# Product-key experts on one core: matmul blocks of one kind in stretches of four, weights in pairs between them

## The chip, the cores and the metric

The kernel runs on one core of a Trainium2 chip. The metric is the device time of one execution in microseconds (us), the median of several runs. A NeuronCore has a matrix engine (TensorE, PE in the profile, with its weight loads as PEld), a vector engine (VectorE, DVE), a scalar engine (ScalarE, ACT), a general engine (GpSimd, POOL) and an engine that starts transfers (SyncE, SP). Each works through its own queue in order; they meet at semaphores. TensorE writes only to PSUM, here eight banks of 128 x 512 float32.

## The reference

The program is a block of four layers over x (4 sequences of 512 tokens, 256 features): two attentions with gates, a mixture of head experts, and at the end the product-key experts, which is the stage that this change touches:

```python
xn = _rmsnorm(x, norm_w)                       # after a layer norm
q = (xn @ w_q.T).reshape(b, t, H, 2, DK)       # H = 8 heads
sim1 = jnp.einsum('bthd,hkd->bthk', q[..., 0, :], keys[:, :, 0, :])   # 64 keys
sim2 = jnp.einsum('bthd,hkd->bthk', q[..., 1, :], keys[:, :, 1, :])
s1, i1 = jax.lax.top_k(sim1, K)                # K = 8
s2, i2 = jax.lax.top_k(sim2, K)
all_sc = (s1[..., :, None] + s2[..., None, :]).reshape(b, t, H, K * K)
fs, pk = jax.lax.top_k(all_sc, K)              # 8 of 64 pairs
fi = jnp.take_along_axis(all_idx, pk, axis=-1) # one of 4096 experts
hidden = jax.nn.gelu(jnp.einsum('btd,bthkd->bthk', xn, expert_down[fi]))
hidden = hidden * jax.nn.relu(fs)
return jnp.einsum('bthk,bthkd->btd', hidden, expert_up[fi])
```

Each token so picks 64 experts of 4096, each with one row of a down and one row of an up matrix.

## The kernel before

The expert stage (`product_key_experts`) gathers nothing. It runs in 16 turns, one for each tile of 128 tokens, and computes the hidden value of **all** 4096 experts, multiplies it by a dense matrix of weights that is zero where an expert was not picked, and multiplies the product by the up matrix. The 4096 experts are 128 x 32: 32 columns j, in eight blocks of four.

TensorE's work of a turn i (function `turn` of the tensor block, L2465):

- `hidden(i + 1, ..., n)`, n = 0 to 7, L2423: block n of down matrix times the normed tile of the **next** turn, in float32, 8 matmuls of 128 columns; the trace has 16 instructions for them. It writes one of two banks in turn, and waits until ScalarE has taken that bank's last block through the gelu.
- `weights(i, n)`, L2440: 24 matmuls in bfloat16, 64 columns each. They turn the picks of 16 tokens (n picks the 16) into their dense weights, from one-hot matrices that VectorE made. Blocks 2c and 2c+1 use the one-hots `c` (0 to 3), for which there are two buffers. The result goes to one of three banks, and a block waits until VectorE has used that bank's last content.
- `spend(i - 1, ..., n)`, L2450: block n of weighted hidden values of the **last** turn times the up matrix, float32, 4 matmuls of 256 columns, 8 instructions in the trace. Block 0 waits for the last multiplication of the turn before.
- `turn_x(i + 2)` (L2387), the transposing of the tile after the next, and `compare(i + 2)` (L2397), its similarities with all keys, 8 instructions of 512 columns, which use the two banks of `hidden`. So `hidden` 4 and 5 wait until ScalarE has copied them. ScalarE in its turn copies them only when `largest_places` of tile i + 1 has ended.
- `turn_picks(i + 1)` (L2407): the transposing of the next tile's picks. It waits for the last step of the ranking (43 steps, the last at L2277).

VectorE's work of a turn (L2630): `apply(i, n)` (L2603), the multiplication of weights block n with the hidden values; `onehots(i, 2)` and `(i, 3)`, and at the end those of the next turn, `(i + 1, 0)` and `(i + 1, 1)`, after `split_score(i + 1)` (L2564, L2567); one-hots are three instructions (L2580, L2585, L2591). `update` (L2609) adds a finished tile to x. The ranking `topk` has six parts: part 0 is `largest` (16 MAX8, L2191) for tile i + 2; parts 1 to 5, for tile i + 1, are `largest_places` (16 searches, L2287), and the four parts of `rank`: 2 (pair sums and 8 MAX8, from L2240), 3 (8 searches from L2252, then small steps to L2259), 4 and 5 (L2228, L2233, L2235 each; 5 ends at L2277). In turns 2 to 9 the layer norm of the last batch lies here too, one part a turn (`late`).

The last turns differ by `ahead`, the number of tiles that are still ahead: turn 15 has no `hidden`, no comparison and no ranking, and after it the eight `spend` of tile 15 follow. Turn 0 has no `spend`.

The order is written out by hand. TensorE's in a middle turn is, before the change, with H, S, W for the three kinds of block, X, C, P for `turn_x`, `compare`, `turn_picks`:

H0 S0 S1 H1 W0 W1 S2 H2 W2 S3 H3 W3 X S4 C W4 H4 S5 H5 W5 S6 H6 W6 S7 H7 P W7

Of the kernel before, what the change touches and what calls it, by code (L numbers as in the profile page):

```python
# [25 lines left out]
B, S, D = 4, 512, 256  # L26
# [89 lines left out]
def build(nc, a, out):  # L116
    with ExitStack() as ctx:
# [41 lines left out]
        b_attention(nc, a, m)  # L159
        c_attention(nc, a, m)  # L160
        product_key_experts(nc, a, m)
        epilogue(nc, out, m)

# [2127 lines left out]
def product_key_experts(nc, a, m):  # L2291
# [10 lines left out]
    NB, BP = 8, 8  # L2302
# [14 lines left out]
    e = m["D"]  # L2317
# [10 lines left out]
    c_out, c_y, c_bo = m["C.out_made"], m["work"][:, 15616:15872], m["work"][:, 15872:16128]  # L2328
    every_other = ident.rearrange("p (n two) -> p two n", two=2)
    SELECT, PICK = 3, 7  # L2330
    late, LATE, LATE_FROM = e.norm, 4, 2

    with ExitStack() as ctx:
        def sig(what, per):
# [2 lines left out]
        def sem(what):  # L2337
            return ctx.enter_context(nc.semaphore("D_" + what))

        consts, c_added = sem("consts"), sem("last_attention_added")  # L2340
# [14 lines left out]
        with nc.Block() as block:  # L2355
# [24 lines left out]
            def _(eng):  # L2380
                def turn_x(i):

                    eng.wait_ge(staged.sem, staged.at(i, 1))
                    if i == 1:
                        eng.wait_ge(selt_ready.sem, selt_ready.at(0, 2))
                    for c in range(KC):
                        last = eng.transpose(XP[:, c * P:(c + 1) * P], xstage[:, c * P:(c + 1) * P], ident[:, :])  # L2387
                    last.then_inc(xt_made.sem, 1)

                def compare(i, par):  # L2390

                    eng.wait_ge(xt_ready.sem, xt_ready.at(i, 1))
                    if i >= 2:
                        eng.wait_ge(h_ready.sem, h_ready.at(i - 1, SELECT + 1))
                    for n in range(2):
                        for kc in range(KC):
                            last = eng.matmul(WP[n] if i == 1 else HP[n][:, :], xnT[par][:, kc, :], simw[:, kc, n * 512:(n + 1) * 512],  # L2397
                                              start=(kc == 0), stop=(kc == KC - 1))
                        last.then_inc(sim_made.sem, 1)
# [11 lines left out]
                def hidden(i, par, n):  # L2411

                    if i and i < NT - 1 and n in (SELECT + 1, SELECT + 2):
                        eng.wait_ge(sim_ready.sem, sim_ready.at(i + 1, n - SELECT))
                    if i == 0 and n % 2 == 0:
                        eng.wait_ge(s[f"down_loaded_{n // 2}"], 16)
                    if n >= 2:
                        eng.wait_ge(h_ready.sem, h_ready.at(i, n - 1))
                    elif h_ready.due(i - 1, ELO // NJ - 1 + n):
                        eng.wait_ge(h_ready.sem, h_ready.at(i - 1, ELO // NJ - 1 + n))  # L2420
                    for q in range(NJ):
                        for kc in range(KC):
                            last = eng.matmul(HP[n % 2][:, q * P:(q + 1) * P], down[:, (n * NJ + q) * KC + kc, :],  # L2423
                                              xnT[par][:, kc, :], start=(kc == 0), stop=(kc == KC - 1))
                    last.then_inc(h_made.sem, 1)

                def weights(i, n):

                    if n % 2 == 0:
                        eng.wait_ge(hot_ready.sem, hot_ready.at(i, n // 2 + 1))  # L2430
                    if n >= 3:
                        eng.wait_ge(g_ready.sem, g_ready.at(i, n - 2))
                    elif g_ready.due(i - 1, (7, 8, 6)[n]):
                        eng.wait_ge(g_ready.sem, g_ready.at(i - 1, (7, 8, 6)[n]))
                    c = n // 2 % 2
                    for q in range(BP):
                        at = n % 2 * BP + q
                        dst = WP[n % 3].rearrange("p (j t) -> p j t", t=TW)[:, :, 2 * q:2 * q + 2]
                        for f in range(3):
                            last = eng.matmul(dst, hot[:, c, at, :], lot[c][:, at, f, :], start=(f == 0), stop=(f == 2))  # L2440
                    last.then_inc(w_made.sem, 1)

                def spend(i, par, n):

                    if n == 0:
                        eng.wait_ge(g_ready.sem, g_ready.at(i, NB))
                        if turn_done.due(i - 2, 1):
                            eng.wait_ge(turn_done.sem, turn_done.at(i - 2, 1))
                    for j in range(n * NJ, (n + 1) * NJ):
                        last = eng.matmul(UPP[par][:, 0:D], G[par][:, j, :], up[:, j, :],  # L2450
                                          start=(j == 0), stop=(j == ELO - 1))
                    if n == NB - 1:
                        last.then_inc(up_made.sem, 1)
# [9 lines left out]
                eng.wait_ge(sim_ready.sem, sim_ready.at(1, 2))  # L2463

                def turn(i, par, ahead):  # L2465
                    for n in range(NB):
                        if n == 0 and ahead >= 1:
                            hidden(i + 1, 1 - par, n)
                        if i:
                            spend(i - 1, 1 - par, n)  # L2470
                        if n == SELECT + 1:
                            if ahead >= 2:
                                compare(i + 2, par)
                            weights(i, n)
                        if n and ahead >= 1:
                            hidden(i + 1, 1 - par, n)
                        if n == PICK and ahead >= 1:
                            turn_picks(i + 1)
                        if n == 1:
                            weights(i, 0)  # L2480
                        if n and n != SELECT + 1:
                            weights(i, n)
                        if n == SELECT and ahead >= 2:
                            turn_x(i + 2)

                turns(turn)
                for n in range(NB):
# [58 lines left out]
            def _(eng):  # L2546
# [4 lines left out]
                def topk(i, part):  # L2551

                    if part == 0:
                        largest(eng, m, i)
                    elif part == 1:
                        largest_places(eng, m, i)
                    else:
                        rank(eng, m, i, part, selt_made)
# [37 lines left out]
                def apply(i, par, n):  # L2596

                    if n == 0:
                        eng.wait_ge(h_ready.sem, h_ready.at(i, NB))
                        if up_made.due(i - 2, 1):  # L2600
                            eng.wait_ge(up_made.sem, up_made.at(i - 2, 1))
                    eng.wait_ge(w_made.sem, w_made.at(i, n + 1))
                    eng.tensor_tensor(G[par][:, :, n * TW:(n + 1) * TW], WP[n % 3].rearrange("p (j t) -> p j t", t=TW),  # L2603
                                      Hg[par][:, :, n * TW:(n + 1) * TW], ALU.mult).then_inc(g_ready.sem, 1)

                def update(i, par):
                    eng.wait_ge(up_made.sem, up_made.at(i, 1))
                    xt = x[:, i, :]
                    eng.scalar_tensor_tensor(out=xt, in0=UPP[par][:, 0:D], scalar=gate, in1=xt, op0=ALU.mult, op1=ALU.add  # L2609
                                             ).then_inc(turn_done.sem, 1)  # L2610
# [13 lines left out]
                onehots(0, 1)  # L2624
                topk(1, 0)
                topk(1, 1)
                PARTS = {0: 1, 1: 2, 2: 3, 4: 4, 5: 5}
                FIRST_PARTS = {0: 2, 2: 3, 4: 4, 5: 5}

                def turn(i, par, ahead):  # L2630
                    for n in range(NB):
                        apply(i, par, n)
                        if n in (1, 3):
                            onehots(i, 2 + n // 2)
                        if n == 2 and i >= 2:
                            update(i - 2, par)
                        parts = PARTS if i else FIRST_PARTS
                        if ahead >= 1 and n in parts:
                            topk(i + 1, parts[n])
                        if n == LATE and LATE_FROM <= i < LATE_FROM + late.parts:  # L2640
                            if i == LATE_FROM:
                                eng.wait_ge(c_added, 2)
                            late.on_vector(eng, B - 1, i - LATE_FROM)
                        if ahead >= 2 and n == PICK - 1:
                            topk(i + 2, 0)
                        if ahead >= 1 and n == PICK:
                            split_score(i + 1)
                            onehots(i + 1, 0)
                            onehots(i + 1, 1)

                turns(turn)
                update(NT - 2, 0)
# [46 lines left out]
```

## Time and profile before

| what | value |
|---|---|
| runs | 2201.64, 2198.76, 2201.66 us; median 2201.64 |
| the profiled execution | 2201.63 us, its span 2199.8 us, mean granted clock 0.998 |
| TensorE busy | 2140.0 us, 97% of the span |
| VectorE busy | 1671.2 us, 76% |
| ScalarE busy | 791.6 us, 36% |
| expert stage | from about 1592 us to the end |

How to read it: an engine's rows carry the start and the duration of an instruction or of a merged run of them. Matmuls are pipelined, so the duration of one is longer than its distance from the next; how long a block holds TensorE is the distance from its start to the start of what follows. A row's bracket names the idle time before it and the instruction that ended it. "PEclk" is the granted TensorE clock as a share of 2.4 GHz.

### The profile page before, as it was taken

To read this page: it belongs to the slowest core of one execution; us is meant where nothing else is said; L and a number is where in the kernel's file an instruction comes from. 1 tells how busy PE (TensorE), PEld (TensorE's weight loads), DVE (VectorE), ACT (ScalarE), POOL (GpSimd) and SP (SyncE) were. 2 spreads that over 40 slices of the span, in tenths; PEclk is the share of its full clock that TensorE was granted. 3 is DMA by queue.
4 is the path that set the end of the run, shared out by engine and by line. 5 is a ranking of instruction groups with operands and counts; after the bars stand their busy time and mean duration, and the time that the engine had idled before them with its cause. 6 is when DMAs were issued, how large, how long until landed. Compare 5 with 4: busy or idle time off the path is not lost. (4 is left out here: it accounts for less than half of the span.)

```text
span 2199.8 us, 44678 instructions
## 1 busy us (share of the span) xinstructions
PE 2140.0 (97%) x17740; PEld 1443.5 (66%) x17740; DVE 1671.2 (76%) x4463; ACT 791.6 (36%) x1687; POOL 270.2 (12%) x515
## 2 busy tenths in 40 slices
PE   7999989999999999999999999999999999999998
PEld 3555544446746746775556555556689989898997
DVE  6888886776576576536887787877788988889896
ACT  4877772312302302303554554555422111211210
POOL 4866643000000000000000001000000000000000
PEclk9999999999999999999999999999999999999999
DMA  5112104000000003001000000001200000000000
GB/s 181 33 46 52 34 22 158 1 1 1 1 0 1 1 1 115 1 1 51 1 1 1 1 1 1 1 1 51 94 12 2 2 11 2 1 11 1 2 11 10
DMA packets 26207, 50.66 MB, mean 23 GB/s; under 512 B 6032, under 2 KB 14480, under 8 KB 24976
## 3 DMA queue, kind: packets, MB, share of 16 engines
q1 hardware_dynamic: 26000, 47.81, 6.6%
q8 instruction: 141, 2.31, 0.4%
q14 instruction: 66, 0.54, 0.1%
HBM read 37.57 MB, written 2.10 MB: 18 GB/s over the span
## 5 line engine op out<-in xcount | busy, mean ns | idle before, releaser
L2423 PE MATMUL banks<-work,big 128*128 128x128 f32 x2016 | 247.5, 276 | 0.9 <-DMA big<-in_D_up 0.9
L626 ACT ACTIVATE work<-banks,work 128x512 f32<-128x512 f32 x256 | 174.8, 687 | 202.2 <-DVE work L746 202.2
L2423 PEld LDWEIGHTS banks<-work,big 128*128 128x128 f32 x2016 | 241.3, 192 | 5.9 <-DMA big<-in_D_up 1.1
L1121 PE MATMUL banks<-big,work 128*128 128x256 f32 x1024 | 241.2, 379 | 0.0
L1045 PE MATMUL banks<-big,work 128*128 128x512 f32 x512 | 226.6, 596 | 0.0
L2520 ACT ACTIVATE work<-banks 128x512 f32<-128x512 f32 x126 | 75.3, 597 | 398.5 <-PE banks L2423 398.5
L1121 PEld LDWEIGHTS banks<-big,work 128*128 128x128 f32 x1024 | 195.0, 190 | 33.9 <-issue 1.9
L1045 PEld LDWEIGHTS banks<-big,work 128*128 128x128 f32 x512 | 95.5, 190 | 113.8 <-issue 112.8
L1963 ACT ACTIVATE work<-work 128x512 f32<-128x512 f32 x256 | 164.3, 711 | 0.1
L746 DVE TENSOR_REDUCE work<-banks 128x2 f32<-128x1024 f32 x128 | 150.5, 1217 | 7.7 <-PE banks L478 7.7
L1343 DVE CUSTOM_DVE_ANT_0 work<-banks,work 128x512 f32<-128x512 f32 (+3 forms) x128 | 57.6, 488 | 121.5 <-PE banks L1061 109.4
L1872 PEld LDWEIGHTS banks<-ident,work 64*128 64x128 f32 x2048 | 76.4, 140 | 99.9 <-ACT work L1963 69.4
L494 PEld LDWEIGHTS banks<-ident,work 64*128 64x128 f32 x2048 | 74.0, 139 | 89.1 <-issue 51.5
L1228 ACT ACTIVATE work<-work 128x512 f32<-128x512 f32 (+3 forms) x128 | 70.8, 554 | 168.4 <-DVE work L1343 168.3
L1312 DVE TENSOR_TENSOR work<-banks,work 128x512 f32<-128x512 f32 x128 | 87.9, 690 | 52.1 <-PE banks L1045 51.6
L478 PE MATMUL banks<-work 64*128 64x256 f32 x1024 | 124.6, 383 | 0.9 <-DVE work L739 0.9
L2450 PE MATMUL banks<-big,wab 128*128 128x256 f32 x512 | 122.6, 385 | 0.8 <-DVE wab L2603 0.8
L2450 PE MATMUL banks<-big,work 128*128 128x256 f32 x512 | 121.2, 384 | 0.8 <-DVE work L2603 0.8
L507 PE MATMUL banks<-big,wc 128*64 128x512 f32 x512 | 116.9, 598 | 3.4 <-ACT wc L647 2.9
L764 DVE COPY big<-banks 128x512 f32<-128x512 f32 x128 | 87.7, 685 | 38.9 <-PE banks L494 38.7
L755 DVE TENSOR_SCALAR work<-work 128x512 f32<-128x512 f32 x256 | 113.0, 484 | 4.5
L2591 DVE TENSOR_TENSOR wc<-wc,work 128x3072 bf16<-128x3072 bf16 x64 | 112.1, 1752 | 0.0
(256 smaller groups left out, 3782.1 us busy)
## 6 DMA issues: line engine op xcount, KB each, us to landing
work<-work SPq DMA_DIRECT2D x168, 32.0 KB, 2.0
big<-in_bias SPq DMA_DIRECT2D x16, 256.0 KB, 3.6
big<-in_B_val SPq DMA_DIRECT2D x8, 512.0 KB, 5.4
big<-in_B_out SPq DMA_DIRECT2D x1, 4096.0 KB, 16.7
big<-in_D_downT SPq DMA_DIRECT2D x4, 1024.0 KB, 5.6
big<-in_D_up SPq DMA_DIRECT2D x1, 4096.0 KB, 15.6
wc<-in_ctxT SPq DMA_DIRECT2D x1, 2048.0 KB, 8.0
wab<-in_L_ffn_w_q SPq DMA_DIRECT2D x1, 2048.0 KB, 9.5
```

Of the source, the lines that this page charges most:

```text
L478: last = eng.matmul(SB[i][:, j, c * 256:(c + 1) * 256], qT[r, t % 2, qt * P:(qt + 1) * P], kT[r, t % 2, c * 256:(c + 1) * 256], start=True ...
L507: last = eng.matmul(FB[0][j * DK:(j + 1) * DK, :], vtok[:, kt, h * DK:(h + 1) * DK], pT[:, (t % 2 * PAIR + j) * QT + kt, :], start=(kt == ...
L626: eng.activation(prob[:, n % NS * PAIR + j, :], SB[n % 2][:, j, :], ACT.Exp, bias=low[:, n % NS, j:j + 1], accum_out=rowsum[:, n % NS, j:j ...
L746: eng.tensor_reduce(low[:, n % NS, :], SB[n % 2], AX.X, ALU.max, negate=True).then_inc(low_ready.sem, 1)
L755: last = eng.tensor_scalar(one, one, rinv[:, n % NS, j:j + 1], None, ALU.mult)
L1045: last = eng.matmul(value_bank(b, n), xnT[:, kc, t * P:(t + 1) * P], w_val[:, kc, h * EB * DK:(h + 1) * EB * DK], start=(kc == 0), stop=(k ...
L1121: last = eng.matmul(XO[qt // 2][:, qt % 2 * D:(qt % 2 + 1) * D], spread[:, c % NG, qt * P:(qt + 1) * P], w_out[:, c, :], start=False, stop ...
L1312: eng.tensor_tensor(scaled[:, n % NG, :].rearrange("p (k e) -> p k e", e=EB), value_bank(b, n).rearrange("p (k e) -> p k e", e=EB), gm[:, ...
L1963: eng.activation(one, one, ACT.Exp, bias=low[:, n % 2, j:j + 1], scale=-1.0).then_inc(p_ready, 1)
L2423: last = eng.matmul(HP[n % 2][:, q * P:(q + 1) * P], down[:, (n * NJ + q) * KC + kc, :], xnT[par][:, kc, :], start=(kc == 0), stop=(kc == ...
L2450: last = eng.matmul(UPP[par][:, 0:D], G[par][:, j, :], up[:, j, :], start=(j == 0), stop=(j == ELO - 1))
L2591: eng.tensor_tensor(lot[b].rearrange("p n f (j two) -> p n f j two", two=2), elo[:, b].rearrange("p n (j two) -> p n j two", two=2).unsque ...
```

## The change

TensorE's turn is put in two halves of four blocks each. In a half, four H stand together, then two W, then four S, then two W. `turn_x` stands behind W1, the comparison behind S3, `turn_picks` behind S7. In the letters from above a middle turn is then:

H0 H1 H2 H3 W0 W1 X S0 S1 S2 S3 C W2 W3 H4 H5 H6 H7 W4 W5 S4 S5 S6 S7 P W6 W7

VectorE's turn is dealt in pairs to match: multiplications 0 and 1, one-hots 2, parts 1 and 2 of the ranking; multiplications 2 and 3, one-hots 3, the update, part 3; multiplications 4 and 5, parts 4 and 5, the layer norm's part, part 0 of the tile after the next; multiplications 6 and 7, the score's split and two one-hots. ScalarE's code is the same, and so is every instruction of TensorE and VectorE; only their order in the queues changes. The diff, with a constant that is no longer used left out:

```diff
                 def turn(i, par, ahead):
-                    for n in range(NB):
-                        if n == 0 and ahead >= 1:
-                            hidden(i + 1, 1 - par, n)
-                        if i:
-                            spend(i - 1, 1 - par, n)
-                        if n == SELECT + 1:
-                            if ahead >= 2:
-                                compare(i + 2, par)
-                            weights(i, n)
-                        if n and ahead >= 1:
-                            hidden(i + 1, 1 - par, n)
-                        if n == PICK and ahead >= 1:
-                            turn_picks(i + 1)
-                        if n == 1:
-                            weights(i, 0)
-                        if n and n != SELECT + 1:
-                            weights(i, n)
-                        if n == SELECT and ahead >= 2:
-                            turn_x(i + 2)
+                    for half in (range(NB // 2), range(NB // 2, NB)):
+                        for n in half:
+                            if ahead >= 1:
+                                hidden(i + 1, 1 - par, n)
+                        weights(i, half[0])
+                        weights(i, half[1])
+                        if half[0] == 0 and ahead >= 2:
+                            turn_x(i + 2)
+                        for n in half:
+                            if i:
+                                spend(i - 1, 1 - par, n)
+                        if half[0] == 0 and ahead >= 2:
+                            compare(i + 2, par)
+                        if half[0] and ahead >= 1:
+                            turn_picks(i + 1)
+                        weights(i, half[2])
+                        weights(i, half[3])
...
-                PARTS = {0: 1, 1: 2, 2: 3, 4: 4, 5: 5}
-                FIRST_PARTS = {0: 2, 2: 3, 4: 4, 5: 5}
-
                 def turn(i, par, ahead):
-                    for n in range(NB):
-                        apply(i, par, n)
-                        if n in (1, 3):
-                            onehots(i, 2 + n // 2)
-                        if n == 2 and i >= 2:
-                            update(i - 2, par)
-                        parts = PARTS if i else FIRST_PARTS
-                        if ahead >= 1 and n in parts:
-                            topk(i + 1, parts[n])
...
+                    apply(i, par, 0)
+                    apply(i, par, 1)
+                    onehots(i, 2)
+                    if ahead >= 1:
+                        if i:
+                            topk(i + 1, 1)
+                        topk(i + 1, 2)
+                    apply(i, par, 2)
+                    apply(i, par, 3)
+                    onehots(i, 3)
+                    if i >= 2:
+                        update(i - 2, par)
+                    if ahead >= 1:
+                        topk(i + 1, 3)
+                    apply(i, par, 4)
+                    apply(i, par, 5)
+                    if ahead >= 1:
+                        topk(i + 1, 4)
+                        topk(i + 1, 5)
+                    if LATE_FROM <= i < LATE_FROM + late.parts:
...
+                    if ahead >= 2:
+                        topk(i + 2, 0)
+                    apply(i, par, 6)
+                    apply(i, par, 7)
+                    if ahead >= 1:
+                        split_score(i + 1)
+                        onehots(i + 1, 0)
+                        onehots(i + 1, 1)
```

## Rows read from the trace of the kernel before

**Rows 1.** The page's first part: busy time, share of the span, instructions.

```profile
span 2199.8 us, 44678 instructions
PE 2140.0 (97%) x17740; PEld 1443.5 (66%) x17740; DVE 1671.2 (76%) x4463; ACT 791.6 (36%) x1687; POOL 270.2 (12%) x515
```

**Rows 2.** Busy time by stretch; behind the engines the granted clock, DMA share, GB/s.

```profile
1640.00:2120.00 480.00, 480.00 (x5060) 430.49 (x5059) 417.54 (x1496) 94.22 (x188) 5.84 (x26) 1.00 0.02 5
2160.00:2199.80 39.80, 34.60 (x320) 29.67 (x320) 21.45 (x29) 0.00 (x0) 0.00 (x0) 1.00 0.04 14
```

**Rows 3.** The waits of TensorE from 1600 us on: total, times, longest.

```profile
PE banks L2440 <- DVE wc L2591: 1.0, 1, 1.0
```

**Rows 4.** Timeline of TensorE, a middle turn: start, duration, line, shapes, count.

```profile
1893.73 2.03 PE L2423 MATMUL banks<-work,big 128*128 128x128 f32 x16
1895.60 3.62 PE L2450 MATMUL banks<-big,work 128*128 128x256 f32 x16
1899.05 1.95 PE L2423 MATMUL banks<-work,big 128*128 128x128 f32 x16
1900.84 1.56 PE L2440 MATMUL banks<-wc 128*128 128x64 bf16 x48
1902.24 1.97 PE L2450 MATMUL banks<-big,work 128*128 128x256 f32 x8
1904.05 1.95 PE L2423 MATMUL banks<-work,big 128*128 128x128 f32 x16
...
1929.12 1.95 PE L2423 MATMUL banks<-work,big 128*128 128x128 f32 x16
1931.00 0.57 PE L2407 MATMUL banks<-ident,work 128*64 128x64 f32 x12
...
1932.21 1.92 PE L2423 MATMUL banks<-work,big 128*128 128x128 f32 x15
```

**Rows 5.** Timeline of TensorE, turn 0 and the start of turn 1.

```profile
1602.35 1.56 PE L2440 MATMUL banks<-wc 128*128 128x64 bf16 x48
...
1608.88 0.42 PE L2387 MATMUL banks<-ident,work 128*128 128x128 f32 x2
...
1614.25 3.82 PE L2423 MATMUL banks<-work,big 128*128 128x128 f32 x32
1617.90 0.86 PE L2440 MATMUL banks<-wc 128*128 128x64 bf16 x24
...
1624.35 2.03 PE L2423 MATMUL banks<-work,big 128*128 128x128 f32 x16
```

**Rows 6.** Timeline of VectorE, turn 0.

```profile
1603.93 0.68 DVE L2240 TENSOR_TENSOR wab<-work 128x512 f32<-128x512 f32 x1
...
1609.81 0.68 DVE L2603 TENSOR_TENSOR wab<-banks,work 128x512 f32<-128x512 f32 x1
...
1612.71 0.68 DVE L2603 TENSOR_TENSOR wab<-banks,work 128x512 f32<-128x512 f32 x1
...
1617.31 0.42 DVE L2228 TENSOR_TENSOR wab<-work 128x512 bf16<-128x512 bf16 x1
...
1622.07 0.69 DVE L2603 TENSOR_TENSOR wab<-banks,work 128x512 f32<-128x512 f32 x1
```

**Rows 7.** Timeline of TensorE, end of turn 14, turn 15 and after it.

```profile
2158.80 0.87 PE L2440 MATMUL banks<-wc 128*128 128x64 bf16 x24
2160.46 3.72 PE L2450 MATMUL banks<-big,wab 128*128 128x256 f32 x16 [0.78 <-DVE wab L2603]
2165.21 1.57 PE L2440 MATMUL banks<-wc 128*128 128x64 bf16 x48 [1.03 <-DVE wc L2591]
...
2182.82 14.08 PE L2450 MATMUL banks<-big,work 128*128 128x256 f32 x64 [0.78 <-DVE work L2603]
```

**Rows 8.** Early in the first attention: TensorE's timeline, then busy time by stretch.

```profile
32.52 1.12 PE L1872 MATMUL banks<-ident,work 64*128 64x64 f32 x16 [1.21 <-ACT wc L1957]
...
33.00:39.00 6.00, 6.00 (x39) 3.07 (x37) 4.68 (x13) 4.08 (x7) 0.00 (x0) 0.50 0.69 218
```

More of the change, by code:

```diff
@@ L2330, in product_key_experts @@
     SELECT, PICK = 3, 7
-    late, LATE, LATE_FROM = e.norm, 4, 2
+    late, LATE_FROM = e.norm, 2
     with ExitStack() as ctx:
@@ L2626, in _ @@
                 topk(1, 1)
-                PARTS = {0: 1, 1: 2, 2: 3, 4: 4, 5: 5}
-                FIRST_PARTS = {0: 2, 2: 3, 4: 4, 5: 5}
                 def turn(i, par, ahead):
-                    for n in range(NB):
-                        apply(i, par, n)
-                        if n in (1, 3):
-                            onehots(i, 2 + n // 2)
-                        if n == 2 and i >= 2:
-                            update(i - 2, par)
-                        parts = PARTS if i else FIRST_PARTS
-                        if ahead >= 1 and n in parts:
-                            topk(i + 1, parts[n])
[L2640 to L2649, printed above, removed]
+                    apply(i, par, 0)
@@ new lines, in turn @@
+                    apply(i, par, 5)
[3 more added lines that the diff above has]
+                    if LATE_FROM <= i < LATE_FROM + late.parts:
+                        if i == LATE_FROM:
+                            eng.wait_ge(c_added, 2)
+                        late.on_vector(eng, B - 1, i - LATE_FROM)
+                    if ahead >= 2:
+                        topk(i + 2, 0)
+                    apply(i, par, 6)
+                    apply(i, par, 7)
```

## The prediction

> **What bounds the kernel now.** I read four views in this order. The page's first part: TensorE is busy 2140.0 us of a span of 2199.8 us [rows 1]. The busy time by stretch: from 1640 to 2120 us, twelve and a half turns of the expert stage, TensorE is busy 480.00 of 480.00 us at a granted clock of 1.00, VectorE 417.54 us (87%) and ScalarE 94.22 us (20%) [rows 2]. The reader is to see that no engine but TensorE sets the pace there, and that VectorE is near enough to take over. The waits from 1600 us on: TensorE waits for VectorE's one-hots 1.0 us in all [rows 3]. Last the timeline of TensorE in one turn, where starts can be subtracted. One turn goes from 1893.73 to 1932.21, 38.48 us [rows 4], and the pieces add up to that with no gap. I call a block of the down matmuls H (L2423, 16 instructions), of the weights W (L2440, 24), of the up matmuls S (L2450, 8), the comparison C (L2397), the turning of x X (L2387) and that of the picks P (L2407).
>
> **The price of a piece depends on what precedes it.** S directly after W lasts 1902.24 to 1904.05, 1.81 us; two S after H last 1895.60 to 1899.05, so 1.73 each. H after S lasts 1899.05 to 1900.84, 1.79 (1.78 in most turns); H after W 1893.73 to 1895.60, 1.87. The H before P takes 1929.12 to 1931.00, 1.88 [rows 4]. So a float32 block behind the short bfloat16 ones pays 0.08 to 0.09 us. Two W in a row cost 1900.84 to 1902.24, 1.40, exactly twice one: nothing is gained inside a pair. H directly behind H costs no less: H4 and H5 of turn 0, 32 instructions from 1614.25 to 1617.90 [rows 5], 3.65 us, are 1.87 + 1.78.
>
> **Steady turns, 1 to 14.** No matmul is added or removed; only the neighbours change. Before, W is followed by S four times a turn (S2, S3, S6, S7), by H twice (H4, H0 of the next turn) and by X once. After it: S once (S4), H twice (H4, H0), X once. Three W-to-S steps go: 3 x 0.08 = 0.24 us a turn. P moves from behind H7 to behind S7. No row shows S before P; if the 0.10 us that the H before P pays [rows 4] belonged to the H, it would go too, if to P, it stays. Bounds 0.24 and 0.34 us a turn; I take 0.24, since nothing in H changes before P, while P's matmuls have another shape (128x64): it looks like P's price. 14 x 0.24 = **3.4 us gained** (to 4.8). The Trainium skill (TensorE: Matmul & The Clock Gate, section on LDWEIGHTS) gives a weight load as its columns over 1.2 GHz, 107 ns for 128 columns; if one whole unhidden load were the price of a step, an estimate from that page would be 3 x 0.107 x 14 = 4.5 us. The rows have 0.08, so I keep 3.4.
>
> Does VectorE keep up in a steady turn? From the start of W4: W5 is done 1.40 us later and VectorE starts about 0.2 us after that; then come multiplication 5 and the ranking's parts 4 and 5. Before, those three take 1617.31 to 1622.07 (in another order), 4.76 us [rows 6], so the picks are ready at 6.4 to 6.5. TensorE wants them after W4, W5 and four S: 1.40 + 1.81 + 3 x 1.73 = 8.40. Slack 1.9 us. At the turn's end: multiplication 7, the score's split and the first one-hots take 5.71 us from the end of W7 (below), against four H, 7.2 us: slack 1.5. ScalarE may copy the comparison only when the ranking's part 1 has ended, and H4 waits for the copy. VectorE, from the end of W7: 5.7, second one-hots with two multiplications 4.60 (1612.71 to 1617.31 [rows 6]), one-hots again at most 4.6, and 16 searches, at most twice the 2.3 of part 3, which has 8: under 19.5. The copy needs about 0.6; TensorE comes to H4 at 7.2 + 1.40 + 0.25 + 7.0 + 3.4 + 1.4 = 20.6. So the steady turns lose nothing. ScalarE at 20% has its work in the same order; its H evacuations (0.60 us) fit behind 1.78.
>
> **Turn 0 has no S, and there the cover is gone.** Before, it runs W0 at 1602.35 and ends with H0 of turn 1 at 1624.35 [rows 5]. After, two more H (2 x 1.78) stand before W0: W0 at 1605.91, X at 1607.31. From X to the end of the W behind the comparison it is 1608.88 to 1614.25 = 5.37 [rows 5], a wait for ScalarE included, so 4.67 to the start of that W: W2 at 1611.98. Then 1.40, four H (1.87 + 3 x 1.78 = 7.21): W4 at 1620.59, and TensorE is through W5 at 1621.99. It now wants P, and the picks of tile 1 are not there. VectorE starts multiplication 1 at 1607.5, when W1 is done. Until W4 is there it does multiplications 1 to 3, two one-hots and parts 2 and 3: part 2, a multiplication and one-hots are 1603.93 to 1609.81, 5.88; a multiplication, one-hots and a multiplication 1612.71 to 1617.31, 4.60; part 3 is 1609.81 to 1612.71 less a multiplication of 0.61, 2.29 [rows 6]. That ends at 1620.3, so it waits for W4 itself. W5 is done for VectorE at 1622.2; multiplication 5 and parts 4 and 5 take the 4.76 from above: P at about 1627.0. **TensorE stands 5.1 us**, with P, W6, W7 and all of turn 1 queued behind the wait; P 0.50 and two W 1.40 end at 1629.0 against 1624.35. **Cost 4.6 us.** Before, parts 4 and 5 stood between multiplications 4, 5 and 6, each beside an H.
>
> **Turn 15 has no H.** Before: W7 of turn 14 ends at 2159.50, two S run, and W0 of turn 15 waits for its one-hots until 2165.21 [rows 7], 5.71 us after. That chain is VectorE's and stays (multiplication 7, split, one-hots; L2591 is the releaser in the row). After, the S of turn 14 stand behind W0 and W1, so those 3.46 us of S no longer fill the wait. From W0 on: 1.40, S 1.81 + 5.19, two pairs of W 2.80, S 7.00, a pair 1.40, and 0.94 for multiplication 7: 20.54, together 26.25 us. (VectorE is in time for W4: from W0 on it has two one-hots and two multiplications, 4.60 + 3.4 = 8.0 us, and W4 comes at 1.40 + 7.00 + 1.40 = 9.8.) Before it is 2182.82 - 2159.50 = 23.32 [rows 7]. **Cost 2.9 us.** The last eight S are unchanged.
>
> **Sum at an unchanged clock.** 4.6 + 2.9 - 3.4 = +4.1 (with the 0.34 a turn: +2.7). The profiled execution took 2201.63 us for a span of 2199.8, and the median of the runs is 2201.64, so nothing is to be converted: 2205.8 us (2204.3 at the better bound).
>
> **The pauses and the clock.** The two pauses, 5.1 and 5.7 us, are longer than any wait of TensorE that the trace has behind its start. What follows them may run at a lower clock. The nearest rows: around 32 us TensorE runs small turning matmuls with a wait of 1.21 us between them, and from 33 to 39 us the granted clock is 0.50 (the 1.2 GHz level) while the engine is busy 6.00 of 6.00 us [rows 8]. That cost up to 3 us of full-speed work for the 6 us, and I bound each pause by 0 and 3. The waits of 0.78 and 1.03 us between dense blocks in the last turn [rows 7] cost no clock, which is 1.00 from 2160 us on [rows 2]. A pause of over 5 us is emptier than the thin stretch that lost it, so I hold a fall after at least one of the pauses to be likely, and take 2.2 us for both together, between one fall of half that length and two. The Trainium skill (same page, section "Why this matters for your kernels") says that an idle gap between matmul bursts sends the array back to the half clock; no row has such a gap, and the early stretch points the same way.
>
> **Forecast:** 2205.8 + 2.2 = 2208.0 us, slower by 0.3%.
>
> **Rivals.** (a) The clock holds in both pauses: 2205.8, or 2204.3 with P's 0.10 saved; +0.12 to 0.19%, not to be told from no change. For it: the short waits of rows 7 left the clock at 1.00, and the early stretch that lost it lay behind a row of small matmuls, not behind dense ones. Against it: the length of the pauses beside those of rows 7 and 8. (b) The cover is better than I walk it: if ranking in turn 0 ended within the time of W4 and W5, TensorE would not stand, 4.6 us go and the time is 2201.2 or, with 0.34 a turn, 2199.8. It decides on parts 4 and 5 starting over 5 us sooner, and they stand behind W5 in VectorE's own order; hardly possible. (c) VectorE becomes the bound in steady turns. Slack is 1.5 to 1.9 us, less in turns 2 and 3, where statistics of the layer norm come on top; should a wait I missed eat it and 0.5 us more, 14 x 0.5 = 7 us come on top: 2215. Against it, VectorE has 13% idle and stands waiting for W4 in my walk, so it begins each half in step.
>
> **Chances.** Forecast (a fall after one pause or both) 0.60, (a) 0.30, (b) 0.04, (c) 0.06. About 0.2%, 4.4 us, is what a measurement can tell from no change: the line lies at 2206.0. Slower by more: 0.60 + 0.06 = 0.66. Within: 0.30. Faster: 0.04, as even (b) hardly passes the lower line. Range: two full falls give 2205.8 + 6 = 2211.8; the lower end is (a) at its better bound less a little for the spread of the runs shown (2198.76 to 2201.66): 2203.5 to 2212.0.
>
> **What the next profile would show.** A turn of 38.24 (or 38.14) us with no wait of TensorE; S after W once a turn; a wait of 5.1 us before P near 1622 us, released by the ranking (L2277), and one of 5.7 us before W near 2160, released by L2591; a granted clock of 0.50 behind one of them. Wrong would be: waits of TensorE in turns 1 to 14, P without a wait in turn 0, or H or S blocks whose length changed inside their stretches.

## The result, and the profile after

The changed kernel takes 2208.21 us, the kernel before beside it 2199.88 us: a ratio of 1.0038, 95% interval 1.0028 to 1.0047. It is slower by 8.3 us. The forecast was slower, 2208.0 us; against the 2201.64 us that it started from it said 6.4 us.

The profiled execution of the changed kernel took 2206.67 us. The page's first part:

```profile
span 2204.9 us, 44634 instructions
PE 2131.7 (97%) x17707; PEld 1440.5 (65%) x17740; DVE 1675.8 (76%) x4463; ACT 792.3 (36%) x1687; POOL 269.0 (12%) x515
```

TensorE's share is still 97% [rows 1]; the page alone would not show what went wrong. The two profiled spans differ by only 5.1 us. The reason lies far from the change: the low clock at 33 to 39 us [rows 8] is absent here. Busy time by stretch, the granted clock third from the right:

```profile
33.00:39.00 6.00, 5.51 (x53) 2.48 (x52) 5.55 (x15) 5.08 (x8) 0.00 (x0) 1.00 0.68 220
1640.00:2120.00 480.00, 480.00 (x5076) 428.75 (x5075) 423.32 (x1522) 94.59 (x186) 5.11 (x26) 1.00 0.02 5
```

So everything after it is some 3 us earlier, before the change can act. In the twelve profiles of this study the down blocks of the first turn begin anywhere from 1595.7 to 1599.0 us. They begin at 1595.7 to 1595.8 in the three whose mean granted clock over the first 60 us is 1.00, at 1596.2 to 1597.2 in the six with 0.97, and at 1598.7 to 1599.0 in the three with 0.94, the kernel before among these. This spread of 3 us has nothing to do with the change, so below I also compare by **stage time**: from the first down block behind the wait for the up matrix to the start of the last 64 instructions of the up matmuls. Before it is 1598.67 to 2182.82, 584.15 us. Each stage time is that of one profiled execution.

**A middle turn.** TensorE's timeline of the changed kernel:

```profile
1896.25 7.39 PE L2423 MATMUL banks<-work,big 128*128 128x128 f32 x64
1903.47 1.56 PE L2440 MATMUL banks<-wc 128*128 128x64 bf16 x48
...
1905.12 7.07 PE L2450 MATMUL banks<-big,work 128*128 128x256 f32 x32
1912.03 3.60 PE L2397 MATMUL banks<-work 128*128 128x512 f32 x8
...
1925.49 7.15 PE L2450 MATMUL banks<-big,work 128*128 128x256 f32 x32
1932.58 0.57 PE L2407 MATMUL banks<-ident,work 128*64 128x64 f32 x12
...
1934.49 5.71 PE L2423 MATMUL banks<-work,big 128*128 128x128 f32 x49
```

The turn is 1896.25 to 1934.49, 38.24 us, where it was 38.48 [rows 4]: the gain is there, to the hundredth. Four S behind X take 6.91, four S between W and P 7.09, which is 0.08 for the step from W and 0.10 in front of P.

**The waits of TensorE** from 1600 us on, where there was one of 1.0 us [rows 3], and then its timeline at the two places:

```profile
PE banks L2440 <- DVE wc L2589: 5.5, 1, 5.5
PE banks L2407 <- DVE work L2277: 4.9, 1, 4.9
```

```profile
1595.75 7.41 PE L2423 MATMUL banks<-work,big 128*128 128x128 f32 x64 [0.83 <-DMA big<-in_D_up]
...
1617.70 1.56 PE L2440 MATMUL banks<-wc 128*128 128x64 bf16 x48
1624.21 0.91 PE L2407 MATMUL banks<-ident,work 128*64 128x64 f32 x12 [4.95 <-DVE work L2277]
1625.05 2.74 PE L2440 MATMUL banks<-wc 128*128 128x64 bf16 x48
1627.60 8.31 PE L2423 MATMUL banks<-work,big 128*128 128x128 f32 x64
1635.75 1.56 PE L2440 MATMUL banks<-wc 128*128 128x64 bf16 x48
...
2158.95 1.57 PE L2440 MATMUL banks<-wc 128*128 128x64 bf16 x48
2166.06 2.74 PE L2440 MATMUL banks<-wc 128*128 128x64 bf16 x48 [5.53 <-DVE wc L2589]
2168.61 7.26 PE L2450 MATMUL banks<-big,wab 128*128 128x256 f32 x32
...
2187.84 14.08 PE L2450 MATMUL banks<-big,work 128*128 128x256 f32 x64 [0.79 <-DVE work L2601]
```

One wait stands in turn 0 in front of the picks and one in turn 15 in front of the first weights. Behind each a block that lasts 1.40 us elsewhere (48 instructions of L2440) holds TensorE 2.55 us. The clock in the stretches around the waits:

```profile
1620.00:1622.50 2.50, 0.00 (x0) 0.00 (x0) 2.33 (x6) 0.00 (x0) 0.00 (x0) 1.00 0.00 0
1623.50:1629.00 5.50, 4.79 (x66) 4.68 (x67) 4.45 (x25) 0.98 (x3) 0.00 (x0) 0.50 0.01 1
1630.00:1635.00 5.00, 5.00 (x47) 5.00 (x47) 5.00 (x6) 1.79 (x3) 0.00 (x0) 1.00 0.02 3
...
2166.00:2167.00 1.00, 0.94 (x18) 0.95 (x19) 1.00 (x2) 0.00 (x0) 0.00 (x0) 0.50 0.00 0
```

In turn 0 it was 1.00 until 1622.5 us, was at 0.50 when TensorE began again, and came back while it worked; in turn 15 the weights began at 0.50. The account between the two traces:

| piece | before | after | difference | of it low clock |
|---|---|---|---|---|
| turn 0, from its first H to H0 of turn 1 | 25.68 | 31.85 | +6.17 | 1.47 |
| turns 1 to 14, to the end of W7 | 535.15 | 532.76 | -2.39 | 0.93 |
| from there to the last eight S | 23.32 | 27.48 | +4.16 | 1.25 |
| stage time | 584.15 | 592.09 | +7.94 | 3.65 |

The last column is the length of the blocks behind a pause less that of the same blocks in the kernel with filled pauses (the first experiment): P, W6, W7 3.39 against 1.92; the four H behind them 8.15 against 7.22; W0, W1 of turn 15 2.55 against 1.41, and the four S behind them 7.10 against 6.99.

### The profile page after: what moved, and what is told of

Its sections match the earlier page's. It is cut to its first block and busy times, and to the rows that moved or that the text cites. A ratio compares the mean times of both kernels' runs of the same rounds, so it can differ in the third digit from the quotient of the medians.

```text
span 2204.9 us, 44634 instructions
## 1 busy us (share of the span) xinstructions
PE 2131.7 (97%) x17707; PEld 1440.5 (65%) x17740; DVE 1675.8 (76%) x4463; ACT 792.3 (36%) x1687; POOL 269.0 (12%) x515
## 5 line engine op out<-in xcount | busy, mean ns | idle before, releaser
L1121 PE MATMUL banks<-big,work 128*128 128x256 f32 x1024 | 241.2, 379 | 3.6 <-issue 3.3
L2423 PE MATMUL banks<-work,big 128*128 128x128 f32 x2016 | 234.0, 277 | 0.8 <-DMA big<-in_D_up 0.8
L2423 PEld LDWEIGHTS banks<-work,big 128*128 128x128 f32 x2016 | 228.7, 193 | 1.6 <-DMA big<-in_D_up 1.0
L2450 PE MATMUL banks<-big,work 128*128 128x256 f32 x512 | 113.7, 381 | 0.8 <-DVE work L2601 0.8
L2450 PE MATMUL banks<-big,wab 128*128 128x256 f32 x512 | 114.0, 381 | 0.0
```

Of the source, the lines that this page charges most:

```text
L1121: last = eng.matmul(XO[qt // 2][:, qt % 2 * D:(qt % 2 + 1) * D], spread[:, c % NG, qt * P:(qt + 1) * P], w_out[:, c, :], start=False, stop ...
```

## The experiments

Three theories had to be told apart: that all of the loss lies in turns 0 and 15; that the pauses themselves lower the clock, and not the pairs of small matmuls; and that the gain of the middle turns is a count of places where a float32 block follows a weights block.

**Pauses filled.** The changed kernel with matmuls added in both pauses (L2469 in its trace), whose result nobody reads:

```diff
+                    if i == NT - 1:
+                        eng.wait_ge(h_ready.sem, h_ready.at(i, NB))
+                        fill(HP[0], 6)
...
+                        if half[0] and i == 0:
+                            eng.wait_ge(c_added, 1)
+                            fill(UPP[1], 5)
                         if half[0] and ahead >= 1:
                             turn_picks(i + 1)
```

> The changed kernel with TensorE kept at work in its two pauses: before the picks of turn 0 ten added float32 matmuls of 256 columns (5 x 0.86 = 4.3 us of the 4.95 us pause) into a bank that nobody reads, and twelve (5.2 us of 5.5) before the first weights of turn 15. Theory (the pauses themselves make the clock fall): the granted clock stays 1.00 behind both places, the picks and the weights there run at their usual lengths, and the time is the sum at an unchanged clock, about 4.2 us over the kernel before; the runs lie as close together as those of the kernel before. Rival (the clock falls from what follows the pauses, the small matmuls of picks and weights in pairs, or from the new order as such): 0.50 behind the same places and the time of the changed kernel, about 8 us over before.

Measured: 2204.16 us against 2199.68, ratio 1.0018 (1.0009 to 1.0027). TensorE's timeline at the two places:

```profile
1620.23 4.56 PE L2469 MATMUL banks<-work,big 128*128 128x256 f32 x20
1625.34 0.57 PE L2407 MATMUL banks<-ident,work 128*64 128x64 f32 x12 [0.55 <-DVE work L2277]
...
1627.26 7.39 PE L2423 MATMUL banks<-work,big 128*128 128x128 f32 x64
...
2159.10 5.43 PE L2469 MATMUL banks<-work,big 128*128 128x256 f32 x24
2164.80 1.57 PE L2440 MATMUL banks<-wc 128*128 128x64 bf16 x48 [0.27 <-DVE wc L2601]
2166.21 7.15 PE L2450 MATMUL banks<-big,wab 128*128 128x256 f32 x32
```

The blocks behind have their usual lengths, the granted clock is 1.00 from 1620 to 1635 and from 2159 to 2175 us, and the stage time (1596.89 to 2185.34) is 588.45, 4.30 over before. More work made the kernel about 4 us faster than the changed one. The pauses lower the clock, and the sum at an unchanged clock is 4.3 us. The runs of this kernel spread over 5.1 us (2202.63 to 2207.75), the changed kernel's over 6.5, those of before here over 5.5: that part of the expectation says little.

**Both end turns as before.** The old order of both engines for `i in (0, NT - 1)`, the new one between:

```diff
+                def turn(i, par, ahead):
+                    (turn_old if i in (0, NT - 1) else turn_new)(i, par, ahead)
```

> The order of both engines as before in turns 0 and 15, the new one in turns 1 to 14. Theory (all of the loss lies in the first and the last turn): no pause over 1.1 us, clock 1.00 in the stage, a turn of 38.24 us against 38.48, and 14 x 0.24 = 3.4 us faster than before (ratio 0.9985). Rival (the new order costs something in the middle turns that the picture of one turn hides, or the gain there is given back): no faster than before.

Measured: 2196.46 us, ratio 0.9985 (0.9976 to 0.9994), 3.2 us faster by the medians where 3.4 was expected. The stage time is 580.82 (1597.16 to 2177.98), 3.33 less than before. The longest wait of TensorE in the stage is the 1.0 us that before had too. The middle turns give all that was worked out.

**One end turn at a time.**

> Only turn 0 in the order before, both engines; turns 1 to 15 new. Theory: the pause in front of the picks of turn 0 is gone and with it the low clock behind it, the pause of 5.5 us in turn 15 stays with its low clock: 4.7 + 2.4 = 7 us less than the changed kernel at most, so about before + 0.8 (the clock in turn 15 included). Rival (the wait for the picks comes from turn 1's start too): a wait of TensorE in turn 1.

> Only turn 15 in the order before; turns 0 to 14 new. Theory: the wait in turn 15 shrinks from 5.5 to 1.0 us, the clock there stays 1.00, 2.9 + 1.2 = 4.1 us less than the changed kernel, so about before + 3.8 (the low clock behind the pause of turn 0 included, some 2.4). Rival (turn 15 is bound by VectorE): no change against the changed kernel.

Measured: with turn 0 as before 2201.16 us, ratio 1.0008 (0.9999 to 1.0018); with turn 15 as before 2202.65, ratio 1.0013 (1.0003 to 1.0023), beside 2199.65. By the medians this is 1.5 and 3.0 us over before, where 0.8 and 3.8 were expected; the first of the two can't be told from no change. By stage time it is 585.45 (+1.30) and 588.32 (+4.17). Of the two long waits the former keeps only the 5.5 us in front of W0 of turn 15, the latter only the 4.9 us in front of the picks. Each pause goes with its own turn, and each kept its low clock: in the former the four S of turn 15 take 7.55 us, in the latter the four H of turn 1 take 8.55. The sums are 2.9 - 3.3 + 1.7 = 1.3 and 4.7 - 3.3 + 2.8 = 4.2, where 1.7 and 2.8 are the low clock's cost read as above.

**A last turn of its own.** Turn 0 as before, turns 1 to 14 new, and for turn 15:

```diff
+                def turn_last(i, par, ahead):
+                    for spent, made in ((range(4), range(4)), ((4, 5), (4, 5)), ((6, 7), (6, 7))):
+                        for n in spent:
+                            spend(i - 1, 1 - par, n)
+                        for n in made:
+                            weights(i, n)
```

> As the run with both end turns restored, but turn 15 in an order of its own: four up blocks of tile 14 ahead of the weights (S0 to S3, W0 to W3, S4 S5, W4 W5, S6 S7, W6 W7), with VectorE's new order. The four S, 7 us, cover the 5.7 us that the one-hots take, where the order before has two S (3.5 us) and a wait. Theory: no wait of TensorE in turn 15 but 0.8 us at its start, 1.7 us less than with the old last turn, 5.1 us faster than before (ratio 0.9977). Rival (the last turn is bound by VectorE's chain of one-hots whatever TensorE's order): the same time as with both end turns restored.

Measured: **2193.87 us against 2199.68, ratio 0.9978 (0.9969 to 0.9987)**, 5.8 us faster than before by the medians, where 5.1 was expected. It is the fastest kernel of the study by its median, but the two variants of it below lie too close to be told from it. Its timeline at the end:

```profile
2154.20 7.17 PE L2450 MATMUL banks<-big,wab 128*128 128x256 f32 x32 [0.78 <-DVE wab L2633]
2161.21 2.96 PE L2440 MATMUL banks<-wc 128*128 128x64 bf16 x96
2164.01 3.70 PE L2450 MATMUL banks<-big,wab 128*128 128x256 f32 x16
...
2174.82 14.08 PE L2450 MATMUL banks<-big,work 128*128 128x256 f32 x64 [0.78 <-DVE work L2633]
```

The weights stand behind four S and wait for nothing. The stage time is 579.09, 5.06 less than before, 1.73 less than with the old last turn, as worked out.

**VectorE dealt as before.** TensorE's new order, VectorE's old one in all turns:

> TensorE's new order with VectorE's old dealing in all turns. Theory (the pairing of VectorE's work is needed only because the weights come in pairs; with the old dealing a part 0 of the ranking stands between multiplications 6 and 7, which both wait for the end of the turn, and the first one-hots come too late for W0): a wait of 0.5 us in front of W0 in each of turns 1 to 14, a turn of 38.7 us, 7 us slower than the changed kernel, 15 us slower than before. Rival (VectorE has slack enough for either dealing): the turn stays at 38.24.

Measured: 2212.77 us, ratio 1.0062 (1.0045 to 1.0079). The waits, and a middle turn:

```profile
PE banks L2440 <- DVE wc L2589: 8.8, 14, 5.5
```

```profile
1898.79 7.39 PE L2423 MATMUL banks<-work,big 128*128 128x128 f32 x64
1906.43 1.57 PE L2440 MATMUL banks<-wc 128*128 128x64 bf16 x48 [0.25 <-DVE wc L2589]
...
1937.46 2.70 PE L2423 MATMUL banks<-work,big 128*128 128x128 f32 x22
```

Thirteen waits of 0.25 us, half of what was expected, have joined the one of 5.5, one in each of turns 2 to 14. H0 to W0 is 7.64 us instead of 7.22, and the turn 38.67, as worked out. A wait costs more than its row says, because the row of four H lasts 7.39 us but TensorE usually starts the next block after 7.22; with a wait the 0.17 of overlap goes too. The stage time is 598.26, 6.2 more than the changed kernel's: 13 x 0.43 is 5.6, turns 1 to 14 together take 5.7 more, and 0.6 is a longer low clock in turn 15 (four S in 7.69 us where the changed kernel has 7.10). Between the medians it is 13.1 us over before where 15 was expected. The pairing of VectorE's work is a needed half of the change, as the slack of 1.5 us in front of W0 says: the old dealing puts about 2 us of ranking between multiplications 6 and 7.

**A pair split.** Two more places a turn where S follows W:

```diff
                         for n in half:
+                            if n == half[2] and 0 < i < NT - 1:
+                                weights(i, n)
                             if i:
                                 spend(i - 1, 1 - par, n)
```

> The changed kernel with the second pair of weights of each half split in turns 1 to 14: W2 stands between S1 and S2, W6 between S5 and S6. Two more places per turn where S follows W, the same work. Theory (0.08 us for each place where a float32 block follows W, nothing else): a turn of 38.24 + 0.16 = 38.40 us. Rival (the gain of the new turn is from longer stretches of H or S as such): the split of the S stretches into twos costs more, back to 38.48.

Measured: the turn goes from 1881.29 to 1919.70, 38.41 us, by the timeline from one H4 to the next (2211.3 us in one run):

```profile
1881.29 7.39 PE L2423 MATMUL banks<-work,big 128*128 128x128 f32 x64
...
1889.92 3.70 PE L2450 MATMUL banks<-big,wab 128*128 128x256 f32 x16
1893.46 0.86 PE L2440 MATMUL banks<-wc 128*128 128x64 bf16 x24
1894.15 3.70 PE L2450 MATMUL banks<-big,wab 128*128 128x256 f32 x16
...
1919.70 7.39 PE L2423 MATMUL banks<-work,big 128*128 128x128 f32 x64
```

0.17 more for two places, where 0.16 was expected and the rival said 0.24. It is the count of these places that sets the turn, not the length of the stretches of S; the stretches of H were not split.

**The picks moved.** The best kernel above, with the turning of the picks between W6 and W7, and then behind W7:

> As the run with a last turn of its own, but in turns 1 to 14 the turning of the picks stands between W6 and W7 and not between S7 and W6. Theory (the 0.10 us in front of the picks is a drain of the float32 block ahead, and behind W nothing is paid, as the turning of x pays nothing behind W): 0.10 us less a turn, 1.4 us less in all. Rival (the 0.10 us is the picks' own): the same turn of 38.24 us.

> As the run with a last turn of its own, but in turns 1 to 14 the turning of the picks stands behind W7, ahead of H0 of the next turn. The run with the picks between W6 and W7 showed that their 0.10 us is their own. Theory (only a float32 block directly behind W pays 0.08 to 0.09 us, and any block between them takes that step away, as the turning of x does): one step less, 0.09 us a turn, 38.15 us, 1.2 us less in all than with the last turn of its own, 6.3 us faster than before (ratio 0.9971). Rival (the one-hots come 0.7 us later with it and eat their slack of 1.5 us in front of W0, or the picks' matmuls, as short as the weights', leave the same step to H0): a turn of 38.24 us or a wait in front of W0.

Measured: 2195.42 us, ratio 0.9981 (0.9972 to 0.9990), and 2194.85, ratio 0.9976 (0.9967 to 0.9985). Here both theories fell, and the rivals that say the turn stays the same held. The former kernel's turn, then the latter's:

```profile
1890.39 0.86 PE L2440 MATMUL banks<-wc 128*128 128x64 bf16 x24
1891.18 0.57 PE L2407 MATMUL banks<-ident,work 128*64 128x64 f32 x12
```

```profile
1887.63 1.56 PE L2440 MATMUL banks<-wc 128*128 128x64 bf16 x48
1889.13 0.57 PE L2407 MATMUL banks<-ident,work 128*64 128x64 f32 x12
1889.63 7.41 PE L2423 MATMUL banks<-work,big 128*128 128x128 f32 x64
1896.88 1.56 PE L2440 MATMUL banks<-wc 128*128 128x64 bf16 x48
...
1927.88 7.41 PE L2423 MATMUL banks<-work,big 128*128 128x128 f32 x64
```

W6 to P is 0.79 instead of 0.70 and W6 to P across two W 1.50 instead of 1.40: the 0.09 to 0.10 in front of the picks is paid behind H, S and W alike. And four H behind P take 7.25 us, no less than the 7.22 to 7.23 behind W, so the picks' short matmuls leave the step to H as the weights do. That any block between W and H takes the step away is therefore wrong: the turning of x does so ahead of S, the picks do not ahead of H. Both turns are 38.25. The stage times, 579.09 (1599.00 to 2178.09) and 578.79 (1596.20 to 2174.99), are within 0.3 us of the 579.09 of the kernel that they were made from. The 0.3 lies in turn 15, where the latter's picks take the place of 0.5 us of the wait for the last multiplication.

**Pauses filled in half.**

> The changed kernel with the two pauses filled only in part: six added matmuls in turn 0 (2.6 us, 2.4 left) and six ahead of the weights of turn 15 (2.6 us, 2.9 left). Theory (a pause of 5 us lowers the clock, and one of half that length does not always): 1.00 behind at least one of the two. Rival (any pause beyond that of 1.0 us which left the clock alone in the kernel before lowers it): 0.50 behind both.

Measured (2207.52 us in one run), TensorE's timeline and the clock by stretch:

```profile
1627.48 0.57 PE L2407 MATMUL banks<-ident,work 128*64 128x64 f32 x12 [2.28 <-DVE work L2277]
1627.98 1.57 PE L2440 MATMUL banks<-wc 128*128 128x64 bf16 x48
...
2166.94 2.74 PE L2440 MATMUL banks<-wc 128*128 128x64 bf16 x48 [2.87 <-DVE wc L2601]
```

```profile
1627.00:1632.00 5.00, 4.52 (x83) 4.45 (x84) 4.79 (x27) 1.46 (x4) 0.00 (x0) 1.00 0.01 2
2166.00:2168.00 2.00, 1.06 (x20) 1.06 (x21) 2.00 (x3) 0.00 (x0) 0.00 (x0) 0.58 0.00 0
```

The pause of 2.28 us left the clock at 1.00; the one of 2.87 us lowered it, and it cost what the whole one had cost, 2.55 us for a pair of weights. One execution doesn't show where the line lies, or that there is one line.

## Why the prediction was right

**The middle turns.** 14 x 0.24 = 3.4 us forecast, 3.3 measured, in the changed kernel (2.39 + 0.93) and in the one with both end turns restored (3.33). The choice between 0.24 and 0.34 was right too, and for the reason given: the 0.10 is the picks' own. A whole weight load for each place, the estimate from the Trainium skill (TensorE: Matmul & The Clock Gate, section on LDWEIGHTS), would have been 4.5 us. The rows decide for 0.08 to 0.09 a place. That VectorE keeps up held: no wait in turns 1 to 14, and the dealing as before shows that the slack in front of W0 was real and small.

**Turn 0.** Cost 4.6 forecast; 6.17 less the 1.47 of low clock is 4.70. The walk put the pause at 5.1 us; it is 4.95, with the ranking's last instruction as releaser, as named.

**Turn 15.** 2.9 forecast; 4.16 less 1.25 is 2.91. The wait is 5.53 us, released by the one-hots' last instruction.

**The clock.** The sum without it is slower too (+4.3 us); this term carried the forecast over the prediction's line of 4.4 us, and it is the one that was sized wrong. I took 2.2 us for both pauses; this trace has 3.65, and the single pauses of the experiments 1.7 (turn 15 alone) and 2.8 (turn 0 alone). Eight of eight pauses of about 5 us in the profiles lowered the clock, where I gave only 0.60 to one of the two or both. The forecast came out within 0.3 us of the measured time by luck, because a second size was off the other way: the median of before was 2199.88, not 2201.64, as the first runs had it. The change is +8.3 us by the medians, +7.9 by the stage times, not +6.4. The early stretch [rows 8] was a fair guide to the price of a fall: 0 to 3 us were allowed for each pause, and 1.25 to 2.8 were found. The Trainium skill (same page, section "Why this matters for your kernels") has it that idle time between bursts of matmuls costs the clock. These traces agree, with 0.50 behind each of the eight pauses.

**Rivals.** (a), the clock holds, is what the kernel with filled pauses is: +4.3 by stage time, where 4.1 was worked out. That it is not to be told from no change was too careful, as the interval of that kernel, 1.0009 to 1.0027, lies above 1. (b) and (c) did not come about: TensorE stood 4.95 us in turn 0 and nowhere in turns 1 to 14; (c) is real as a mechanism with the old dealing of VectorE's work.

## What to carry to other kernels

When blocks of a steady loop are regrouped, walk the first and the last turn by themselves: the blocks that are missing there were the cover of somebody's wait, and here two turns of sixteen lost more than twice what the fourteen others won, the low clock not counted. Price a pause of TensorE not by its length alone but with what follows it at half the clock. A new order can often be used where it pays alone: with the old order in turn 0 and one of its own in turn 15 the same change is 0.22% faster instead of 0.38% slower.

## What the runs showed of the hardware

- A pause of TensorE of 4.85 to 5.54 us lowered the granted clock to 0.50 in all eight cases, one of 2.87 us did, and those of 2.28 and 1.03 us did not. Behind it 1.25 to 2.8 us were lost, and pauses of one length did not cost the same: the 5.5 us of turn 15 cost 1.25, 1.7, 1.8 and 2.0 us in four kernels. Matmuls that compute nothing of use, placed in the two pauses, gave 3.6 us of stage time back.
- The long wait at the very start of every trace (10.31 us before) is not counted among these. The granted clock reads 1.00 behind it, yet the 16 instructions of L1764 last 1059 ns each on average, where the 16 of L1774, of the same shapes, last 596 ns some 6 us later. Whether the reading or something else is the reason was not tried.
- The clock's fall near 33 us [rows 8] comes in some executions and not in others, with the same program up to there (granted clock from 33 to 39 us: 0.50 in three profiles, 0.72 in six, 1.00 in three). All that follows comes up to 3 us later with it. Two single profiles differ by that much for no reason of the kernel's.
- A float32 block of H or S costs 0.08 to 0.09 us more behind the weights' bfloat16 blocks of 64 columns than behind another H or S, and H as much behind the picks' float32 matmuls of 64 columns; what exactly is paid there, a weight load that could not start early or something else, was not tried.
